# Four tiles of the first diffusion moved to the head of the second step, with the arrays of X and V exchanged and the first layer's loop reordered

## The chip, the cores and the metric

The kernel runs on one core of a Trainium2 chip. It is written by hand for each engine: TensorE (PE) multiplies, VectorE (DVE), ScalarE (ACT) and GpSimd (POOL) do the rest, and SyncE (SP) issues nearly all DMAs. The metric is the time of one execution in microseconds (us), measured on the device; of several runs the median counts.

## The reference

Inputs are `x` (2048 x 512, float32) and a sparse `adj` (2048 x 2048). Two blocks follow each other, each with a residual: `x = x + L0(relu(layernorm(x)), adj)` and then `x = x + L1(relu(layernorm(x)), adj)`. `L0` is a quantised graph layer: 4-bit activations by 3-bit weights, ReLU, quantised again, and `adj @ support`. `L1` is this, with `X` = `V` = its input, `S` = `adj`:

```python
S = S + jnp.eye(n, dtype=X.dtype)
R = S / jnp.clip(S.sum(axis=1, keepdims=True), 1e-12)
Z = jnp.zeros_like(X)
Xf, Xa = (X, X)
...
for s in range(STEPS):                      # two steps
    A = _adj_from_feats(Xa, W1, W2, W3)
    Xf = R @ Xf
    Xa = A @ Xa
    Z = Z + (Xf @ U1s[s] + Xa @ U2s[s])
Y = X + Z
mu = Y.mean(axis=-1, keepdims=True)
var = Y.var(axis=-1, keepdims=True)
return (Y - mu) * jax.lax.rsqrt(var + LN_EPS) * gamma + beta
```

`_adj_from_feats` makes logits `(Xa W1) W2 (Xa W3)^T`, 2048 x 2048, keeps in each row the largest ones that together hold 0.9 of the softmax, and takes the softmax of what was kept. So each step has a diffusion by the fixed matrix `R` and an attention by `A`.

## The kernel before, in words

The 2048 rows are 16 tiles (`T`) of 128, in four groups (`NG`) of four (`G`). Every float32 operand of a product is split into a high and a low half of float16, and a product is the sum of three: high by high, high by low and low by high. The arrays `XR` and `VR` (128 partitions, 16 tiles, two halves, 512) hold the right-hand sides: `XR` the attention's `X`, `VR` the diffusion's `V`. `V` starts as `X U11`; the first diffusion makes `V = X U10 + R V` of it and the second `R V`, the sum of the two diffusion terms of `Z`. The program has these stages, by the profile's clock:

- *Quantising* (to about 80 us): the layer norm of `x`, the first layer's support `sup`, the split weights.
- *The first layer* (80 to 358 us): a loop over 16 strips of `adj`. For strip `t` ACT makes the high half (`adj_hi`), VectorE the sums of its rows (`key_sums`, line 1310), its low half (line 1313) and the block on its diagonal (`own_block`), TensorE the products with `sup` (lines 658 and 665) and, last of a tile, the one-column product of line 668. VectorE then normalises (lines 1348 to 1360) and writes `XF`; ACT (`x_hi`, line 987) and GpSimd (`x_lo`, line 521) split it into `XR`, TensorE turns the halves (line 700) and makes `U10`, `U11` and the logits' factors of the tile before (`post0` on ACT, lines 1018 and 1021; `pk_lo`, `v_lo` on GpSimd, lines 529 to 536). SP writes the turned and split strip to `adj_parts` in DRAM.
- *Step 1* (358 to 946 us) and *step 2* (946 to 1400 us), each the same program with other constants: a head, then four groups.
- *The end* (1400 to 1460 us): the last layer norm and the output.

In a step, the logits of a group (`logits`, lines 756 and 757 on TensorE, copied by ACT at line 1061, squares at 1068) come two groups ahead, tile by tile. VectorE takes the largest of each row (line 1469, four tiles of a group), ACT the four Exps (`terms`, line 1088), VectorE searches the threshold in four rounds of sums over all four tiles (line 1382), sorts out the last candidates and writes the kept terms and their sums (`settle`, lines 1559 to 1662). TensorE turns the kept terms (line 684), ACT copies their high (1119) and low half (1125), and TensorE multiplies them by `XR` (lines 830 and 833). ACT writes the product out (1148 in step 1, 1152 in step 2). In step 1 the new `X` then goes through `U20`, the new `Phh`, `Plz`, `Khl` (the logits' factors) and `x_parts` in DRAM.

A tile of the diffusion is 48 matmuls (lines 778 and 780) of a strip of `adj_parts`, which SP brings in, by `VR`. ACT scales it out of the bank (`r_out`, line 1100), GpSimd adds the term of before (`r_sum`, line 565), and in step 1 ACT and GpSimd split the sum into halves (lines 1104 and 536), which SP stores to `v_parts`. `VR` can't take the new `V` before the old one is read for the last time, so `V` comes back from DRAM: `v_in` reloads `VR` ahead of the last group's pairs in step 1, `x_in` reloads `XR` at the head of step 2.

The order is written out by hand and each engine runs its part of it. `step_order` puts the logits of group 0, its Exps, one diffusion tile, the logits of group 1 and diffusion tiles 1 to 8 ahead of the groups (`R_FIRST = 9`), and each group begins with `R_BEHIND = (1, 2, 2, 2)` further ones, the last of them behind the turning of the first kept terms. ACT's `group_start` does

```python
                e_hi(t + s * T, 0)
                e_hi(t + s * T, 1)
                if g < NG - 1:
                    terms(s, g + 1)
                    r_out(s, first_r(g) + count - 1, bank_of(g, count - 1))
```

so all four Exps of the next group stand there together. On VectorE the loop over the groups is `first_guess` (with `largest`, the four reductions, at its head), `search`, `settle`. A wait for a semaphore stands on the engine that needs the data; everything behind it in that engine's program waits with it.

## Time and profile before

| | us |
|---|---|
| three runs | 1462.3, 1460.14, 1460.16 |
| median | 1460.16 |
| profiled execution, its own time | 1462.12 |
| its span | 1460.3 |
| TensorE matmuls busy | 1217.0 (83%) |
| VectorE busy | 1098.2 (75%) |
| ACT busy | 611.0 (42%) |
| GpSimd busy | 292.6 (20%) |

The mean clock granted to TensorE is 0.937 of full speed. DMAs move 141.78 MB. The span is the time between the first and the last instruction on the core; the execution's own time is 1.8 us more. A busy share is an average over stages with different limits: the two engines that are busy most are rarely busy to the full at the same time. How long something waits and what ended the wait is read from the timeline of its engine.

### The profile page before, as it was taken

The numbers are of one execution on the slowest core, as the hardware profiler recorded it, in microseconds if no ns is written. First come the engines' busy times: TensorE is split into PE (matmuls) and PEld (weight loads), VectorE is DVE, ScalarE is ACT, GpSimd is POOL, SyncE is SP. The second block draws the span as 40 slices with busy tenths as digits, with TensorE's granted clock in tenths as the row PEclk, the third lists the DMA queues.
The fourth block names the chain that finished last, engine by engine and source line by source line (L and its number), as shares of the span: only waits on it lengthen the run. The fifth ranks groups of instructions, "written<-read, shape, count | busy, mean of one in ns | idle before, by whom it ended". The sixth has DMA issues, their size and how long they took to land.

```text
span 1460.3 us, 18002 instructions
## 1 busy us (share of the span) xinstructions
PE 1217.0 (83%) x6042; PEld 591.4 (40%) x6042; DVE 1098.2 (75%) x1864; ACT 611.0 (42%) x1164; POOL 292.6 (20%) x236
## 2 busy tenths in 40 slices
PE   0658888887779989989989999879999849689792
PEld 0324443443224445445445545424445325345351
DVE  7877666663389899869959800079999999999958
ACT  1635343332771255465544334494046236243130
POOL 6024333332022211121121210101111101102111
PEclk9989999998889999999999999989999979889996
DMA  6134444441214410020030040153440210111165
GB/s 218 49 132 169 166 168 151 173 152 60 88 51 154 156 44 30 32 85 15 31 101 16 30 166 15 45 208 103 157 137 30 66 51 29 66 51 44 44 225 178
DMA packets 57395, 141.78 MB, mean 97 GB/s; under 512 B 9632, under 2 KB 9632, under 8 KB 53216
## 3 DMA queue, kind: packets, MB, share of 16 engines
q1 hardware_dynamic: 57312, 140.81, 27.8%
q8 instruction: 36, 0.59, 0.2%
q14 instruction: 47, 0.39, 0.1%
HBM read 89.67 MB, written 51.12 MB: 96 GB/s over the span
## 4 chain that ended last, share of the span: by engine, by line
PE 46%; DVE 22%; issue 11%; POOL 8%; ACT 8%; DMA 3%; SPq 1%; DVEq 1%; POOLq 1%; ACTq 0%
DVE WS L1382 7%; PE UB L675 6%; PE AB L830 4%; PE AB L778 4%; PE RB L830 4%; PE AB L665 3%; PE RB L675 3%; PE XB L675 3%; PE RB L778 2%; POOL Plz L529 2%; ACT E L1088 2%; POOL RT L565 2%; PE AB L833 2%; PE AB L780 2%; DVE w L1596 2%
## 5 line engine op out<-in xcount | busy, mean ns | idle before, releaser
L1382 DVE SCALAR_TENSOR_TENSOR WS<-E,g 128x2048 bf16<-128x2048 f32 x128 | 315.4, 2515 | 2.0 <-ACT E L1088 0.8
L1469 DVE TENSOR_REDUCE g<-E 128x1 f32<-128x2048 f32 x32 | 72.9, 2278 | 143.1 <-ACT E L1061 143.1
L684 PE MATMUL TB<-ident,E 128*128 128x128 f32 x512 | 81.2, 287 | 72.8 <-ACT turns L1125 45.1
L1125 ACT ACTIVATE turns<-TB 128x512 f16<-128x512 f32 x128 | 75.3, 594 | 155.0 <-PE TB L690 154.8
L830 PE MATMUL AB<-XR,turns 128*128 128x512 f16 x512 | 130.3, 401 | 0.0
L565 POOL TENSOR_TENSOR RT<-RT,AD 128x512 f32<-128x512 f32 x32 | 55.2, 1725 | 361.3 <-ACT RT L1100 361.3
L830 PE MATMUL RB<-XR,turns 128*128 128x512 f16 x512 | 121.0, 379 | 0.0
L778 PE MATMUL RB<-VR,AH 128*128 128x512 f16 x512 | 115.6, 385 | 0.0
L778 PE MATMUL AB<-VR,turns 128*128 128x512 f16 x512 | 114.1, 379 | 0.0
L684 PEld LDWEIGHTS TB<-ident,E 128*128 128x128 f32 x512 | 66.4, 148 | 98.8 <-issue 48.6
L1119 ACT ACTIVATE turns<-TB 128x512 f16<-128x512 f32 x128 | 75.4, 593 | 34.6 <-PE TB L684 34.6
L1559 DVE SCALAR_TENSOR_TENSOR E<-E,g 128x2048 f32<-128x2048 f32 x33 | 79.2, 2432 | 12.6 <-issue 12.4
L665 PE MATMUL AB<-E,turns 128*128 128x512 f16 x256 | 67.1, 410 | 23.3 <-DVE turns L1313 23.3
L580 POOL TENSOR_TENSOR XHL<-WF,XHL 128x512 f16<-128x512 f32 x16 | 28.3, 1768 | 280.2 <-ACT XHL L1140 280.2
L1061 ACT ACTIVATE E<-LB 128x512 f32<-128x512 f32 x128 | 75.6, 599 | 18.8 <-PE LB L757 17.3
L756 PE MATMUL LB<-Khl,Phh 128*128 128x512 f16 x128 | 53.9, 421 | 33.7 <-ACT E L1061 26.0
L1088 ACT ACTIVATE E<-E,nmx 128x2048 f32<-128x2048 f32 x32 | 63.7, 1997 | 31.5 <-DVE nmx L1470 31.5
L778 PEld LDWEIGHTS RB<-VR,AH 128*128 128x128 f16 x512 | 50.7, 99 | 61.3 <-issue 4.0
L830 PEld LDWEIGHTS AB<-XR,turns 128*128 128x128 f16 x512 | 52.5, 103 | 56.5 <-issue 9.9
L778 PEld LDWEIGHTS AB<-VR,turns 128*128 128x128 f16 x512 | 50.1, 98 | 59.8 <-issue 0.4
L1596 DVE MAX8 w<-WS 128x8 f32<-128x2048 f32 x32 | 73.4, 2295 | 1.1
L598 POOL TENSOR_TENSOR UO<-UO,Khl 128x512 f32<-128x512 f32 x16 | 32.5, 2032 | 204.2 <-ACT UO L1152 150.5
(292 smaller groups left out, 2245.5 us busy)
## 6 DMA issues: line engine op xcount, KB each, us to landing
turns<-adj_parts SPq DMA_DIRECT2D x48, 512.0 KB, 3.8
E<-adjT SPq DMA_DIRECT2D x16, 1024.0 KB, 5.1
adj_parts<-turns SPq DMA_DIRECT2D x16, 1024.0 KB, 3.9
AH<-adj_parts SPq DMA_DIRECT2D x16, 512.0 KB, 3.7
z_d<-UO SPq DMA_DIRECT2D x31, 256.0 KB, 2.3
XR<-x SPq DMA_DIRECT2D x4, 1024.0 KB, 12.0
WS<-U SPq DMA_DIRECT2D x4, 1024.0 KB, 5.6
x_d<-E SPq DMA_DIRECT2D x16, 256.0 KB, 2.6
```

The lines of the kernel that those rows point to most:

```text
L565: q.tensor_tensor(RT[:, :], RT[:, :], AD[:, :], ALU.add).then_inc(s_rsum, 1)
L665: mm(AB[:, :], turns[:, h, 1, j, :], sup[:, j, :], start=False, stop=(j == T - 1))
L675: i = mm(dst, a(k), b(k), start=(first and n == 0), stop=(last and n == 3 * KC - 1))
L684: i = mm(bank[:, k * P:(k + 1) * P], src(k), ident32[:, :], is_transpose=True, start=(k == 0), stop=(k == KC - 1), skip_group_check=True)
L778: i = mm(bank[:, :], at_hi[odd][:, j, :], VR[:, j, k % 2, :], start=(k == 0), stop=False)
L830: mm(bank[:, :], ET[:, 0, j, :], XR[:, j, y_, :], start=(j == 0 and y_ == 0), stop=False)
L1061: a(E[:, slot, c * CH:(c + 1) * CH], LB[c % 2][:, :], ACT.Copy, scale=1.0 / (SV * SV), accum_out=ls[:, bass.ds(slot, 1), c:c + 1].rearrang ...
L1088: a(E[:, slot, :], E[:, slot, :], ACT.Exp, bias=nmx[:, slot:slot + 1], accum_out=tot[:, slot:slot + 1]).then_inc(s_exp, 1)
L1119: a(ET[:, 0, c * KC:(c + 1) * KC, :].rearrange("p b c -> p (b c)"), TB[c % 2][:, :], ACT.Copy, scale=SE).then_inc(s_eh, 1)
L1382: return v.scalar_tensor_tensor(junk[t % 2], e, g4[:, k, t:t + 1], e, op, ALU.mult, accum_out=g4[:, F_, t:t + 1])
L1559: return v.scalar_tensor_tensor(E[:, slot, :], E[:, slot, :], g4[:, k, t:t + 1], E[:, slot, :], ALU.is_ge, ALU.mult, accum_out=g4[:, DEN, ...
L1596: ct(v.max(w8[:, t, :], WS[:, :]))
```

## The change

Three things change. (1) Step 1 runs 12 tiles of the first diffusion, step 2 the other four (`R_LATE`) ahead of its own. The arrays trade places: at the head of step 2 `v_in` loads the first 12 tiles of `V` into `XR`, ACT and GpSimd write the last four straight into `XR`, and the second diffusion reads `XR`; `x_in` loads `X` into `VR` once tile 15 of the first diffusion has been read, and the attention of step 2 reads `VR`. All diffusion tiles of a group now stand ahead of its turning, 0, 1, 1, 1 in step 1 and 1, 3, 4, 3 in step 2. (2) The Exps of the next group are divided: two (`EARLY`) in `group_start`, two in the group's tile 0 behind the squares. VectorE does two of the next group's reductions between `search` and `settle`. (3) In the first layer VectorE sums strip `t + 1`, makes its low half and its own block before it waits for the product of strip `t`; ACT's high half of `t + 1` comes ahead of its copies of the turned x, and its half of x (and GpSimd's) ahead of the rest of the tile before; `key_sums` has two buffers. Ahead of the loop strip 0 is summed between two quantising steps, its high half is made before them, and GpSimd makes a U half before the four roots. SP issues loads and stores in the order that this asks for.

The diff, cut to its core:

```diff
 R_FIRST = 9
-R_BEHIND = (1, 2, 2, 2)
+R_LATE = 4
+EARLY = 2
+R_BEHIND = ((0, 1, 1, 1), (1, 3, 4, 3))
 R_HI = 2 * T
 R_ALL = R_HI + T
...
-        X1T, tmp, key_sums, own = misc[:, 0, :], misc[:, 1, :], misc[:, 2, 0:P], misc[:, 2, P:2 * P]
+        X1T, tmp, own = misc[:, 0, :], misc[:, 1, :], misc[:, 2, 2 * P:3 * P]
+        key_sums = misc[:, 2, 0:2 * P].rearrange("p (h c) -> p h c", h=2)
...
+        def step_order(s, logits, terms, r_one, r_span, group_start, pairs, last_post):
             logits(s, 0)
             terms(s, 0)
-            r_tile(s)
-            logits(s, 1)
-            r_tiles(s, 1, R_FIRST)
+            if s == 0:
+                r_one(0, 0)
+                r_span(0, 1, 3)
+                logits(s, 1)
+                r_span(0, 3, R_FIRST)
+            else:
+                r_one(0, T - R_LATE)
+                r_span(0, T - R_LATE + 1, T - 1)
+                logits(s, 1)
+                r_one(0, T - 1)
+                r_one(1, 0)
+                r_span(1, 1, R_FIRST - R_LATE)
             for g in range(NG):
                 group_start(s, g)
...
+            def l0_tile(t, odd):
+                l0_stores(t)
+                at_out(t + 1, odd)
+                adj_in(t + 3)
+                diag_out(t)
+                post0_stores(t - 1)
+
...
             def v_in():
-                sp.wait_ge(s_vout, 16 * T + OPEN)
+                sp.wait_ge(s_vout, 16 * (T - R_LATE) + OPEN)
+                sp.wait_ge(s_u, 2 * T)
+                sp.dma_start(XR[:, 0:T - R_LATE, :, :].rearrange("p t h d -> p t (h d)"),
+                             v_parts[0:T - R_LATE].rearrange("t p h d -> p t (h d)")).then_inc(s_vr, 16)
+
+            def x_in():
+                sp.wait_ge(s_xout, 16 * T)
                 sp.wait_ge(s_r, T)
                 sp.dma_start(VR[:, :, :, :].rearrange("p t h d -> p t (h d)"),
-                             v_parts.rearrange("t p h d -> p t (h d)")).then_inc(s_vr, 16)
-
-            def x_in():
-                sp.wait_ge(s_xout, 16 * T)
-                sp.wait_ge(s_u, 2 * T)
-                sp.dma_start(XR[:, :, :, :].rearrange("p t h d -> p t (h d)"),
                              x_parts.rearrange("t p h d -> p t (h d)")).then_inc(s_xr, 16)
 
...
             def l0_tile(t):
                 l0(t)
+                x_lo(t, of(XR, t))
                 v_lo(t - 1, of(VR, t - 1))
                 pk_lo(t - 1, 0, t - 1, s_vl, t)
-                x_lo(t, of(XR, t))
...
+                vs = XR if rs else VR
+                if rs and isinstance(t, int) and t == 0 and a == 0:
+                    pe.wait_ge(s_vr, 16)
+                    pe.wait_ge(s_vl, 2 * T + OPEN)
...
+                xs = XR if qq < T else VR
...
                 a(UO[:, :], UB[:, :], ACT.Copy, scale=SV / (SX * SW)).then_inc(s_ue, 1)
+                if more:
+                    x_hi(t + 1)
                 act.wait_ge(s_v, t + 1)
                 act.wait_ge(s_vl, t + OPEN)
                 a(RT[:, :], RB[:, :], ACT.Copy, scale=SV / (SX * SW)).then_inc(s_ve, 1)
...
             def l0_tile(t):
-                xT_halves(t - 1)
                 turn_free(t + 1)
                 adj_hi(t + 1)
+                xT_halves(t - 1)
                 post0(t - 1)
-                x_hi(t)
...
-            def terms(s, g):
+            def terms(s, g, tiles=range(G)):
                 gq = s * NG + g
-                for t in range(G):
+                for t in tiles:
...
+                if rs == 0:
                     act.wait_ge(s_rsum, r + 1)
+                    if late:
+                        act.wait_ge(s_u, 2 * T)
+                        a(XR[:, bass.ds(t, 1), 0, :].rearrange("p o d -> p (o d)"), RT[:, :], ACT.Copy).then_inc(s_vh, 1)
+                    else:
+                        act.wait_ge(s_vout, 16 * t + OPEN)
+                        a(VHL[:, 0, :], RT[:, :], ACT.Copy).then_inc(s_vh, 1)
...
-                a_out(s, g, t, slot, bank_of(g, R_BEHIND[g] + i))
+                if i == 0 and g < NG - 1:
+                    terms(s, g + 1, range(EARLY, G))
+                a_out(s, g, t, slot, bank_of(s, g, R_BEHIND[s][g] + i))
                 if more:
...
                     w_out(t - 1)
+                    if g < NG - 1:
+                        terms(s, g + 1, range(EARLY))
                     pk(t - 1 + T, 1, t - 1, UB)
-                if g:
-                    r_out(s, first_r(g), bank_of(g, 0))
-                if g == NG - 1:
-                    r_out(s, first_r(g) + count - 1, bank_of(g, count - 1))
+                for j, (rs, r) in enumerate(rows):
+                    r_out(rs, r, bank_of(s, g, j))
+                    if s and j == 0 and g < NG - 1:
+                        terms(s, g + 1, range(EARLY))
+                if s + g == 0:
+                    terms(s, 1, range(EARLY))
                 e_hi(t + s * T, 0)
                 e_hi(t + s * T, 1)
-                if g < NG - 1:
-                    terms(s, g + 1)
-                    r_out(s, first_r(g) + count - 1, bank_of(g, count - 1))
...
+            def adj_sums(t):
+                dve.wait_ge(s_raw, 16 * t + 16)
+                v.tensor_reduce(key_sums[:, t % 2, :], raw[:, t % 2, :].rearrange("p (j c) -> p c j", j=T), AX.X,
+                                ALU.add).then_inc(s_part, 1)
+
+            def adj_lo(t):
+                dve.wait_ge(s_ah, t + 1)
+                v.scalar_tensor_tensor(turns[:, t % 2, 1, :, :].rearrange("p t c -> p (t c)"), raw[:, t % 2, :], SA,
+                                       turns[:, t % 2, 0, :, :].rearrange("p t c -> p (t c)"), ALU.mult,
+                                       ALU.subtract).then_inc(s_al, 1)
+
+            quantise_x(0)
+            quantise_x(1)
+            adj_sums(0)
+            quantise_support(0)
+            quantise_x(2)
+            quantise_support(1)
+            quantise_x(3)
+            quantise_support(2)
+            wpk_parts(ch)
+            quantise_support(3)
+            adj_lo(0)
+
...
-            def layer0(t, first=False):
+            def layer0(t, last=False):
                 ct = Chain(dve, c_dve, t * per0 + base)
-                adj_lo(t)
-                own_block(t, ct)
-                if first:
-                    wpk_parts(ct)
+                if not last:
+                    adj_sums(t + 1)
+                    adj_lo(t + 1)
+                    own_block(t + 1, ct)
...
-                    first_guess(g, g + s * NG, ct)
-                    search(g, g + s * NG, ct)
-                    settle(g, g + s * NG, ct)
+                    gq = g + s * NG
+                    if g == 0:
+                        largest(g, gq, ct, slice(0, EARLY))
+                    largest(g, gq, ct, slice(EARLY, None))
+                    first_guess(g, gq, ct)
+                    search(g, gq, ct)
+                    if g < NG - 1:
+                        largest(g + 1, gq + 1, ct, slice(0, EARLY))
+                    settle(g, gq, ct)
```

The first place is VectorE's program around the first layer's loop (the first rows are the end of quantising; `L1310` is the sum of a strip, `L1313` its low half, `L1333` to `L1336` the own block, `L1348` to `L1360` the layer norm down to `XF`). Before:

```order
L1297 TENSOR_SCALAR E<-VR 128x2048
L1310 TENSOR_REDUCE E<-E 128x128
L1313 SCALAR_TENSOR_TENSOR turns<-E,turns 128x2048
L1333 TENSOR_TENSOR E<-E,ident 128x128
L1335 TENSOR_SCALAR diag<-E 128x128
L1336 SCALAR_TENSOR_TENSOR diag<-E,diag 128x128
L1348 TENSOR_SCALAR sc<-LB 128x1
L1359 TENSOR_SCALAR E<-E,mv,sc 128x512
L1360 TENSOR_SCALAR XF<-E 128x512
L1364 COPY sc<-sc 128x1
L1366 UNCONDITIONAL_BRANCH
```

After, where the same lines are 1351, 1356, 1379 to 1382 and 1394 to 1406, and the branch is the head of the loop:

```order
L1356 SCALAR_TENSOR_TENSOR turns<-E,turns 128x2048
L1379 TENSOR_TENSOR E<-E,ident 128x128
L1381 TENSOR_SCALAR diag<-E 128x128
L1382 SCALAR_TENSOR_TENSOR diag<-E,diag 128x128
L1411 UNCONDITIONAL_BRANCH
L1351 TENSOR_REDUCE E<-E 128x128
L1356 SCALAR_TENSOR_TENSOR turns<-E,turns 128x2048
L1379 TENSOR_TENSOR E<-E,ident 128x128
L1381 TENSOR_SCALAR diag<-E 128x128
L1382 SCALAR_TENSOR_TENSOR diag<-E,diag 128x128
L1394 TENSOR_SCALAR sc<-LB 128x1
L1406 TENSOR_SCALAR XF<-E 128x512
```

The sum, low half and block of the next strip stand in the loop ahead of the row that reads the product (`L1394`), and those of strip 0 ahead of the loop.

The second place is ACT's program at the start of group 0 in step 2 (`RT` is a diffusion tile, `E,tot` an Exp, `turns` the halves of kept terms, `squares` those of the logits, `UO` the product of attention tile 0). Before:

```order
L1119 ACTIVATE turns<-TB 128x512 x2
L1088 ACTIVATE E,tot<-E,nmx 128x2048 x4
L1100 ACTIVATE RT<-RB,rinv 128x512
L1125 ACTIVATE turns<-TB 128x512 x2
L1061 ACTIVATE E,ls<-LB 128x512 x2
L1061 ACTIVATE E,ls<-LB 128x512 x2
L1068 ACTIVATE squares,lq<-E 128x1024 x2
L1152 ACTIVATE UO<-AB,rden 128x512
```

After (`L1130` is the diffusion's copy, `L1118` the Exp, `L1154` and `L1160` the two halves, `L1098` the squares, `L1187` the product):

```order
L1130 ACTIVATE RT<-RB,rinv 128x512
L1118 ACTIVATE E,tot<-E,nmx 128x2048 x2
L1154 ACTIVATE turns<-TB 128x512 x2
L1160 ACTIVATE turns<-TB 128x512 x2
L1091 ACTIVATE E,ls<-LB 128x512 x2
L1091 ACTIVATE E,ls<-LB 128x512 x2
L1098 ACTIVATE squares,lq<-E 128x1024 x2
L1118 ACTIVATE E,tot<-E,nmx 128x2048 x2
L1187 ACTIVATE UO<-AB,rden 128x512
```

Two of the four Exps stand ahead of the halves, the other two behind the squares and ahead of the product of tile 0.

The third place is TensorE's program at the end of step 2's head (`LB` is a logits' bank, `RB` and `AB` take diffusion tiles, `TB` turned terms). Before:

```order
L778 MATMUL AB<-VR,turns 128x512 x32
L780 MATMUL AB<-VR,turns 128x512 x16
L805 REGISTER_ALU
L805 COMPARE_AND_BRANCH
L684 MATMUL TB<-ident,E 128x128 x8
L778 MATMUL RB<-VR,AH 128x512 x32
L780 MATMUL RB<-VR,turns 128x512 x16
L690 MATMUL TB<-turns,minus_e 128x512 x2
```

After:

```order
L782 MATMUL LB<-Khl,Phh 128x512
L783 MATMUL LB<-Khl,Plz 128x512
L790 REGISTER_ALU
L790 COMPARE_AND_BRANCH
L808 MATMUL RB<-VR,AH 128x512 x32
L810 MATMUL RB<-VR,turns 128x512 x16
L808 MATMUL AB<-XR,turns 128x512 x32
L810 MATMUL AB<-XR,turns 128x512 x16
L808 MATMUL RB<-XR,AH 128x512 x32
L810 MATMUL RB<-XR,turns 128x512 x16
L808 MATMUL RB<-XR,AH 128x512 x32
L810 MATMUL RB<-XR,turns 128x512 x16
L710 MATMUL TB<-ident,E 128x128 x8
L716 MATMUL TB<-turns,minus_e 128x512 x2
```

Tile 15 of the first diffusion (by `VR`) and tile 0 of the second (by `XR`) follow each other, the loop reads `XR`, and no diffusion tile stands any more between the turning of terms and the taking off of their high halves (`TB<-turns,minus_e`).

## Rows read from the trace of the kernel before

**Rows 1.** Stretches: start:end, us, busy us of PE, PEld, DVE, ACT, POOL, granted clock, DMA, GB/s.

```profile
80.00:347.00 267.00, 222.82 (x1166) 107.27 (x1167) 181.63 (x237) 99.82 (x161) 93.45 (x75) 0.94 0.43 158
504.00:946.00 442.00, 415.64 (x2176) 212.95 (x2174) 286.70 (x534) 212.21 (x440) 76.85 (x64) 0.97 0.15 51
...
1084.00:1380.00 296.00, 239.43 (x1161) 120.42 (x1161) 280.72 (x509) 115.71 (x225) 38.61 (x19) 0.91 0.16 51
```

**Rows 2.** Instructions of line 668: count, least, median and most ns, first and last start.

```profile
L668 PE MATMUL LB<-powc,E x32: 167/209/250, 90.4 to 347.1; 128*128 128x1 f32 x32
```

**Rows 3.** Timeline, TensorE, first layer: start us, us, instruction [idle before <-releaser].

```profile
193.69 0.28 PE L668 MATMUL LB<-powc,E 128*128 128x1 f32 x2
199.68 3.62 PE L658 MATMUL AB<-E,turns 128*128 128x512 f16 x16
204.40 1.04 PE L665 MATMUL AB<-E,turns 128*128 128x512 f16 x4 [1.11 <-DVE turns L1313]
206.86 1.11 PE L700 MATMUL XB<-ident,XR 128*128 128x128 f16 x8 [1.42 <-POOL XR L521]
```

**Rows 4.** Timeline, first layer: VectorE, then ACT, then GpSimd.

```profile
98.25 4.60 DVE L1313 SCALAR_TENSOR_TENSOR turns<-E,turns  x1
...
197.88 0.43 DVE L1360 TENSOR_SCALAR XF<-E 128x512 f32<-128x512 f32 x1
202.07 2.28 DVE L1313 SCALAR_TENSOR_TENSOR turns<-E,turns  x1
...
201.50 0.27 ACT L1018 ACTIVATE Khl<-XB 64x128 f32 x1
208.92 1.90 ACT L987 ACTIVATE turns<-E  x1
...
202.25 2.38 POOL L529 TENSOR_TENSOR Plz<-PKf,Phh 64x128 f32 x1 [0.25 <-POOL VR L536]
```

**Rows 5.** Timeline, TensorE, the end of the first layer.

```profile
358.08 1.01 PE L700 MATMUL XB<-ident,XR 128*128 128x128 f16 x8 [4.83 <-POOL XR L521]
```

**Rows 6.** Timeline, head and groups of step 1: TensorE, then ACT, then VectorE.

```profile
386.82 7.07 PE L778 MATMUL AB<-VR,turns 128*128 128x512 f16 x32
410.34 0.61 PE L756 MATMUL LB<-Khl,Phh 128*128 128x512 f16 x1 [12.13 <-ACT E L1061]
521.09 1.09 PE L684 MATMUL TB<-ident,E 128*128 128x128 f32 x4 [5.43 <-ACT turns L1125]
603.68 0.63 PE L684 MATMUL XB<-ident,XF 128*128 128x128 f32 x4 [1.41 <-ACT XF L1148]
860.74 0.76 PE L684 MATMUL TB<-ident,E 128*128 128x128 f32 x4 [0.29 <-ACT turns L1125]
...
539.13 0.67 ACT L1148 ACTIVATE XF<-AB,rden 128x512 f32<-128x512 f32 x1
...
516.33 2.35 DVE L1382 SCALAR_TENSOR_TENSOR WS<-E,g 128x2048 bf16<-128x2048 f32 x1
596.52 2.35 DVE L1559 SCALAR_TENSOR_TENSOR E<-E,g 128x2048 f32<-128x2048 f32 x1 [1.22 <-issue]
```

**Rows 7.** Groups of instructions by line, whole program: busy us, mean ns, idle before.

```profile
L565 POOL TENSOR_TENSOR RT<-RT,AD 128x512 f32<-128x512 f32 x32 | 55.2, 1725 | 361.3 <-ACT RT L1100 361.3
...
L1061 ACT ACTIVATE E<-LB 128x512 f32<-128x512 f32 x128 | 75.6, 599 | 18.8 <-PE LB L757 17.3
...
L1061 ACT ACTIVATION_READ_ACCUMULATOR E<-LB 128x1 f32 x128 | 26.2, 205 | 0.0
...
L1088 ACT ACTIVATE E<-E,nmx 128x2048 f32<-128x2048 f32 x32 | 63.7, 1997 | 31.5 <-DVE nmx L1470 31.5
```

**Rows 8.** Timeline, start of step 2's group 0: TensorE, VectorE, ACT.

```profile
1084.97 0.63 PE L684 MATMUL TB<-ident,E 128*128 128x128 f32 x4 [0.93 <-ACT turns L1125]
...
1080.82 2.35 DVE L1382 SCALAR_TENSOR_TENSOR WS<-E,g 128x2048 bf16<-128x2048 f32 x1
...
1100.30 0.67 ACT L1152 ACTIVATE UO<-AB,rden 128x512 f32<-128x512 f32 x1
```

320 lines of the change are left out of this document (156 added, 164 removed).

## The prediction, made before the changed kernel ran

> **What bounds the kernel now.** I read the table of stretches first, because one share of busy time says nothing here [rows 1]. From 80 to 347 us (the first layer) TensorE is busy 83% and no engine is full. From 504 to 946 (groups of step 1) TensorE has 416 of 442 us and VectorE 287. From 1084 to 1380 (groups of step 2) it is the reverse: VectorE 281 of 296, TensorE 239. So the same 10 us of matmuls cost time in step 1 and nothing in step 2, as long as they fit into TensorE's 57 idle us there. Then I read the places where the bound changes hands.
>
> *First layer.* The matmul that ends a tile comes first at 90.4 and last at 347.1 [rows 2], 15 periods of 17.1 us. In one of them [rows 3] TensorE waits 1.1 us for VectorE's low half and 1.4 us for GpSimd's low half of x; the cause stands in [rows 4]: after XF (197.88) VectorE still sums the next strip and only then, at 202.07, makes its low half.
>
> *Step 1.* TensorE resumes with tiles at 521.09 after a wait of 5.4 and with those of the last group at 860.74 [rows 6].
>
> *Step 2.* VectorE's search runs without a hole, because ACT has made all four Exps of the next group before [rows 8].
>
> **The change, part by part.** All is counted in the profiled execution (1462.1 us).
>
> *1. First layer, loop.* VectorE now does the sums, low half and own block of strip t+1 before it waits for product t. TensorE's own work per tile: from the end matmul 6.0 us to the next high product (193.69 to 199.68), 16 high and 16 low matmuls at 0.216 each (3.62 = 15 pitches + 0.38), 6.9, eight turnings 0.94: 13.9 us. Do the others keep up? ACT's last copy of keys ends 8.1 us after the end matmul [rows 4]; the copy of x now stands before them, in idle time; then the next high half 1.9, which makes 10.0; low half on VectorE 2.3, 12.4; own block about 1, 13.4. The next end matmul comes at 13.9. It just fits, so I take 13.9. The first period is shorter: the strip is ready, and TensorE has no products of a tile before; it ends with the chain XF, halves of x, turning, about 11.0. With 1.5 for the two U halves that VectorE and GpSimd still fight over: 11.0 + 14 x 13.9 + 1.5 = 207.1 against 256.7. **-49.6.** The moves ahead of it (strip 0 summed while VectorE waits, W parts in another wait, U before the four roots) add 3.7 us of VectorE work to the quantising and take as much from its end; first high product within 1 us of before: 0, range -3 to +2.
>
> Every third tile of before is longer (17.1 on average against 16.7 in the one shown). The Trainium skill (TensorE: Matmul & The Clock Gate, What's actually happening) says that idleness puts the array at 1.2 GHz and activity returns it to 2.4. By that, a loop without waits loses these dips, as in my 13.9; by the row they would stay, 0.4 x 14 = +6, which I keep for the upper end.
>
> *2. Its end.* The last x was turned at 358.08, 11.0 after the last end matmul, behind GpSimd's work on the tile before [rows 5]. Now x goes first; the next in line is ACT, which is busy until +8.1 and then copies the turned x. Before it did that from +12.0. **-3.7.**
>
> *3. Head of step 1.* Before, TensorE did one diffusion tile, then waited 12.1 us in the logits [rows 6] for ACT's four Exps. Now diffusion tiles 1 and 2 stand there. A diffusion tile is 48 x 0.216 = 10.36. In before's clock: three tiles from 386.8 end at 417.9, plus 1.2 for a late transfer; ACT finishes their sums at 422.2; 16 copies of logits at 0.8 (599 + 205 ns) [rows 7] to 434.8; six tiles to 497.0. ACT then needs 0.7 + 1.7 (GpSimd) + 0.6, and the two early Exps 4.0 [rows 7], to 504.3; TensorE resumes with tiles at 506.2, not 521.09. Tile 9, which stood between, is gone from there. **-14.9.** VectorE's first tile is ready at 500.1 (its old 495.3 and two early reductions of 2.4), so it isn't last.
>
> *4. Groups of step 1.* Each group has one diffusion tile fewer, 10.4 us. But what is late next? The search of a group starts in step 1 only with all four Exps, and the last two now stand in ACT's queue behind the squares of tile 0: 18.0 us after TensorE resumes (521.09 to 539.13), then 4.0, then 0.5. From search to first masked tile 80.2 (516.33 to 596.52) [rows 6], plus 4.8 for two early reductions, plus 3.0 until TensorE resumes: 110.5. For the third hand-over tile 0 has no logits, so ACT gets there after 13, and no reduction follows: 100.7. Sum of three: 321.7, against 860.74 - 521.09 = 339.7. **-18.0.** TensorE alone would need 82.6 (to 603.68) + 3.4 for a late copy + 17.3 of tile and rest + 7 = 110.3, so the two are level, and the gain is less than 3 x 10.4 because the wait for the Exps takes the rest. The last group's missing tile lies before 860.74 and is in this sum.
>
> *5. Head of step 2.* Ten diffusion tiles stand before the first turning (12 to 15 of the first, 0 to 5 of the second), nine did. New is a wait: tile 0 of the second needs all V, so after tile 15 TensorE idles for ACT 0.7, GpSimd 1.7, ACT 0.6, GpSimd 1.7 and hops, 5.1. In before's clock: three tiles from 958.6 to 989.7; ACT is behind with three sums, so the logits end at 1005.6; tile 15 to 1016; wait to 1021; six tiles, the first partly cold, 1084.4. ACT: 0.7, then the two early Exps 4.0, both halves: TensorE resumes at 1091, not 1084.97 [rows 8]. X into VR (4 MB) is issued at about 1018 beside this; a strip's transfer may be 2 late. GpSimd's and SP's queues hold the same items in the new order.
>
> *6. The hand-over in step 2.* This is the term against the change. VectorE is done with two reductions, moments and the first two sums of the search at 1080.8, as before. The third needs Exp 3, and that stands in ACT's queue behind the squares of tile 0, 15.3 after TensorE resumes (1084.97 to 1100.30) [rows 8]: 1091 + 15.3 + 2 = 1108, where before it began at 1080.82. **+27.5**, and step 2 is bound by VectorE, so it stays. Later hand-overs: TensorE has 3, 4 and 3 diffusion tiles (31, 41, 31) before the group's turning. After 57.5 of tiles and 31 it is at 1182, VectorE's mask at 1190; then ACT is blocked some 10 us until the late reductions, tiles and 41 end at 1304 against the mask at 1310; then 1398 against 1407. So the four moved tiles lie beside VectorE's work, by 6 to 9 us each time, and cost 0. If that cover is gone, each us is one. The last groups' tail is unchanged.
>
> Sum: -49.6 - 3.7 - 14.9 - 18.0 + 27.5 = -58.7, which makes 1403.4 for an execution like the profiled one; the median of the runs is 2.0 below it: 1401.5, say **1402**.
>
> **The rivals.** *A. The first layer keeps most of its waits.* Its ring VectorE, ACT, VectorE fits with 0.5 us to spare. VectorE's low half took 4.60 instead of 2.28 where GpSimd worked beside it, and GpSimd's Plz 2.38 [rows 4]. If low half and own block meet GpSimd in each tile, the ring is 12.4 + 2.3 + 2.4 = 17.1, no gain; if only the block does, 15.3. For it: two slow rows. Against: in the new order GpSimd's operations start with x at +5.4 and end by +9.3, before the low half. 14 x 1.4 to 14 x 3.2 gives 1422 to 1447. The Trainium skill (GPSIMD Engine Reference, Specifications) states the cause: GpSimd shares its SBUF interfaces with VectorE instructions that have two SBUF inputs, which both are.
>
> *B. No hand-over stall in step 2*, if the two Exps were reached before VectorE asks: 1402 - 27.5 = 1374. Against: the order itself puts squares ahead of them.
>
> *C. Slower than before: TensorE at its lower level.* After the change TensorE is nearly full in some 730 us (207, then 505, then the head of step 2). Its mean granted clock there was 0.94 to 0.97 [rows 1]. From 8% more time in these stretches (58.7 / 730), a mean of about 0.89, all gain is lost. At 0.84, 730 x (0.96 / 0.84 - 1) = +104: 1506. For it: denser work. Against: the stretch 504 to 946 is the densest and has the highest clock, 0.97.
>
> **How the numbers follow.** My forecast gets 61% (own range 1388 to 1418: the 6 us of dips, 5 on each ring, 3 ahead), A 25%, B 9%, C 5%. The range 1384 to 1430 takes in the lower part of A and leaves out B, the rest of A and C. A measurement of this kernel can tell about 0.2% (3 us) from no change. Faster: all but C, 0.95; a change within 3 us needs A in full and a longer stall, 0.01; slower 0.04.
>
> **What would show it.** In the profile after: end matmuls of the first layer 13.9 apart, the last near 297; TensorE's resuming in the last group of step 1 some 86 earlier (860.74 - 53.3 - 32.9 = 774.5); one hole of 25 to 30 us on VectorE in the second search of step 2, released by ACT's Exp; none of that size in the others; 5 us on TensorE before the second diffusion's tile 0. I am wrong if the period is over 15, if VectorE has holes of 10 or more in the two later hand-overs, or if TensorE makes VectorE's masked tiles wait.

## The result and the profile after

The changed kernel takes **1415.16 us** (median of 4 runs, 1413.95 to 1416.03) against 1461.14 before (median of 4). The ratio is 0.9684, 95% interval 0.9668 to 0.9701: 46 us, or 3.2%, faster. The forecast was 1402, its range 1384 to 1430, so the time lies inside, 13 us above the likeliest value. The profiled execution took 1413.95 us, with a span of 1412.2. The comparisons inside the program below are made between this profile and that of before, whose spans differ by 48.1.

The end matmuls of the first layer, which answer [rows 2], and the stretches that answer [rows 1] (start:end, length, busy us of PE, PEld, DVE, ACT, POOL, granted clock, share of DMA, GB/s):

```profile
L694 PE MATMUL LB<-powc,E x32: 167/208/251, 88.0 to 295.8; 128*128 128x1 f32 x32
```

```profile
80.00:296.00 216.00, 207.15 (x1168) 104.14 (x1167) 157.99 (x229) 99.93 (x160) 66.77 (x75) 0.98 0.57 195
504.00:860.00 356.00, 331.08 (x1752) 171.03 (x1749) 252.35 (x459) 170.84 (x360) 57.03 (x51) 0.97 0.10 35
1045.00:1330.00 285.00, 250.56 (x1200) 122.55 (x1198) 270.86 (x488) 100.11 (x188) 35.06 (x21) 0.94 0.22 69
```

TensorE is now busy 96% of the first layer, where it was 83%, and the granted clock there went from 0.94 to 0.98. One whole tile of the loop, TensorE first, then VectorE, then ACT, all in one period of 13.34 (end matmul to end matmul, the pattern of [rows 3, 4]):

```profile
181.65 3.62 PE L684 MATMUL AB<-E,turns 128*128 128x512 f16 x16
185.10 1.03 PE L691 MATMUL AB<-E,turns 128*128 128x512 f16 x4
185.97 0.61 PE L726 MATMUL XB<-ident,XR 128*128 128x128 f16 x8
189.00 0.28 PE L694 MATMUL LB<-powc,E 128*128 128x1 f32 x2
```

```profile
179.87 0.43 DVE L1406 TENSOR_SCALAR XF<-E 128x512 f32<-128x512 f32 x1
180.56 3.74 DVE L1351 TENSOR_REDUCE E<-E  x1 [0.20 <-issue]
185.85 2.29 DVE L1356 SCALAR_TENSOR_TENSOR turns<-E,turns  x1 [1.56 <-ACT turns L1005]
...
183.76 1.91 ACT L1005 ACTIVATE turns<-E  x1
```

No row of TensorE carries a wait: the low half that VectorE makes at 185.85 is that of the *next* strip. VectorE's and ACT's waits have no one behind them.

Step 2 is where the change costs. First the row of TensorE ahead of the second diffusion's tile 0, then ACT, VectorE and TensorE at the start of group 0, which answer [rows 8]:

```profile
938.84 0.58 PE L808 MATMUL AB<-XR,turns 128*128 128x512 f16 x1 [6.29 <-POOL XR L562]
...
1003.48 0.69 ACT L1130 ACTIVATE RT<-RB,rinv 128x512 f32<-128x512 f32 x1 [9.49 <-PE RB L810]
1004.06 1.99 ACT L1118 ACTIVATE E<-E,nmx 128x2048 f32<-128x2048 f32 x1
1008.03 1.06 ACT L1154 ACTIVATE turns<-TB 128x512 f16<-128x512 f32 x2
...
1027.89 1.99 ACT L1118 ACTIVATE E<-E,nmx 128x2048 f32<-128x2048 f32 x1
1031.86 0.67 ACT L1187 ACTIVATE UO<-AB,rden 128x512 f32<-128x512 f32 x1
...
1006.18 2.35 DVE L1430 SCALAR_TENSOR_TENSOR WS<-E,g 128x2048 bf16<-128x2048 f32 x1 [7.81 <-ACT E L1118]
1030.07 2.35 DVE L1430 SCALAR_TENSOR_TENSOR WS<-E,g 128x2048 bf16<-128x2048 f32 x1 [19.26 <-ACT E L1118]
...
1008.67 1.10 PE L716 MATMUL TB<-turns,minus_e 128*128 128x512 f16 x2 [4.36 <-ACT turns L1154]
1010.05 1.09 PE L710 MATMUL TB<-ident,E 128*128 128x128 f32 x4 [0.29 <-ACT turns L1160]
1010.94 3.62 PE L863 MATMUL AB<-VR,turns 128*128 128x512 f16 x8
...
1115.33 1.97 PE L710 MATMUL TB<-ident,E 128*128 128x128 f32 x8 [10.77 <-DVE E L1607]
```

VectorE, the engine that bounds this stage, stands idle twice in one search, 27.1 us in all: before its first sum, for the first Exp, and before its third, for the third, which ACT makes at 1027.89 behind the squares of tile 0. ACT itself waited 9.49 for the last diffusion tile just before the first of these Exps.

Place by place, the same events in both profiles:

| event | before | after | difference | step since the row above | forecast of the step |
|---|---|---|---|---|---|
| first end matmul of the first layer | 90.4 | 88.0 | -2.4 | -2.4 | 0 |
| last end matmul | 347.1 | 295.8 | -51.3 | -48.9 | -49.6 |
| first sum of step 1's search | 405.57 | 351.14 | -54.4 | -3.1 | -3.7 |
| TensorE resumes, group 0 of step 1 | 521.09 | 456.95 | -64.1 | -9.7 | -14.9 |
| TensorE resumes, last group of step 1 | 860.74 | 777.42 | -83.3 | -19.2 | -18.0 |
| TensorE resumes, group 0 of step 2 | 1084.97 | 1010.05 | -74.9 | | |
| third sum of group 1's search, step 2 | 1080.82 | 1030.07 | -50.8 | +32.5 | +27.5 |
| end of the span | 1460.3 | 1412.2 | -48.1 | +2.7 | 0 |

(The forecast's sum of -58.7 is that of the last column.) Without the first layer's part, which earned 54.4 with its lead-in and end, the change costs 6.3 by this table: -9.7 - 19.2 + 32.5 + 2.7. The same by stages: from the first sum of its first search to that of step 2's, step 1 takes 537.4 instead of 566.4, and from there to the last group's first masked tile step 2 takes 439.3 instead of 404.0.

### The profile page after: what moved, and what is told of

It is laid out like the page before. It is cut to its first block, busy times and chain, and to the rows that moved or that the text cites. A ratio compares the mean times of both kernels' runs of the same rounds, so it can differ in the third digit from the quotient of the medians.

```text
span 1412.2 us, 17981 instructions
## 1 busy us (share of the span) xinstructions
PE 1211.1 (86%) x6042; PEld 589.8 (42%) x6042; DVE 1091.7 (77%) x1863; ACT 613.0 (43%) x1164; POOL 273.7 (19%) x236
## 4 chain that ended last, share of the span: by engine, by line
PE 42%; DVE 28%; issue 12%; ACT 9%; DMA 4%; POOL 3%; SPq 1%; DVEq 1%; POOLq 0%; ACTq 0%
DVE WS L1430 10%; PE UB L701 6%; PE RB L863 3%; PE AB L863 3%; PE AB L691 3%; PE AB L684 3%; PE XB L701 3%; ACT E L1118 3%; PE RB L701 3%; DVE w L1644 3%; PE RB L808 2%; PE TB L710 2%; POOL RT L591 2%; DMA AD<-xu_d 2%; PE AB L808 2%
## 5 line engine op out<-in xcount | busy, mean ns | idle before, releaser
L1430 DVE SCALAR_TENSOR_TENSOR WS<-E,g 128x2048 bf16<-128x2048 f32 x128 | 315.1, 2512 | 28.2 <-ACT E L1118 27.1
L1160 ACT ACTIVATE turns<-TB 128x512 f16<-128x512 f32 x128 | 75.7, 594 | 148.9 <-PE TB L716 148.7
L1154 ACT ACTIVATE turns<-TB 128x512 f16<-128x512 f32 x128 | 75.6, 594 | 39.0 <-PE TB L710 38.9
L716 PE MATMUL TB<-turns,minus_e 128*128 128x512 f16 x128 | 52.0, 410 | 33.4 <-ACT turns L1154 33.4
L624 POOL TENSOR_TENSOR UO<-UO,Khl 128x512 f32<-128x512 f32 x16 | 28.5, 1780 | 253.7 <-ACT UO L1187 195.9
L782 PE MATMUL LB<-Khl,Phh 128*128 128x512 f16 x128 | 57.0, 445 | 21.0 <-ACT E L1091 14.0
L684 PE MATMUL AB<-E,turns 128*128 128x512 f16 x256 | 61.3, 395 | 11.9 <-DVE E L1335 5.9
L1098 ACT ACTIVATE squares<-E 128x1024 bf16<-128x1024 f32 x64 | 67.6, 1056 | 2.6
L1118 ACT ACTIVATE E<-E,nmx 128x2048 f32<-128x2048 f32 x32 | 63.6, 1990 | 5.9 <-DVE nmx L1514 5.9
L808 PE MATMUL AB<-XR,turns 128*128 128x512 f16 x256 | 58.8, 390 | 6.3 <-POOL XR L562 6.3
L863 PE MATMUL AB<-VR,turns 128*128 128x512 f16 x256 | 63.4, 393 | 0.0
L1351 DVE TENSOR_REDUCE E<-E (+1 forms) x16 | 59.6, 3723 | 3.0 <-issue 3.0
L863 PE MATMUL AB<-XR,turns 128*128 128x512 f16 x256 | 61.9, 385 | 0.0
L863 PE MATMUL RB<-XR,turns 128*128 128x512 f16 x256 | 61.7, 385 | 0.0
```

What stands on the lines that cost most here:

```text
L684: mm(AB[:, :], turns[:, h, 0, j, :], sup[:, j, :], start=(j == 0), stop=False)
L808: i = mm(bank[:, :], at_hi[odd][:, j, :], vs[:, j, k % 2, :], start=(k == 0), stop=False)
L863: mm(bank[:, :], ET[:, 0, j, :], xs[:, j, y_, :], start=(j == 0 and y_ == 0), stop=False)
L1118: a(E[:, slot, :], E[:, slot, :], ACT.Exp, bias=nmx[:, slot:slot + 1], accum_out=tot[:, slot:slot + 1]).then_inc(s_exp, 1)
L1154: a(ET[:, 0, c * KC:(c + 1) * KC, :].rearrange("p b c -> p (b c)"), TB[c % 2][:, :], ACT.Copy, scale=SE).then_inc(s_eh, 1)
L1160: a(ET[:, 1, c * KC:(c + 1) * KC, :].rearrange("p b c -> p (b c)"), TB[c % 2][:, :], ACT.Copy, scale=SE).then_inc(s_et, 1)
```

## The experiments

Eleven more kernels ran. All medians below are those of a kernel's own 4 or 5 runs, and before was run beside them (medians from 1460.3 to 1462.7).

| kernel | us | ratio to before, 95% interval |
|---|---|---|
| changed kernel | 1415.16 | 0.9684 (0.9668 to 0.9701) |
| first layer's part alone | 1409.17 | 0.9632 (0.9608 to 0.9657) |
| all but the first layer's part | 1472.13 | 1.0082 (1.0050 to 1.0113) |
| changed, four Exps in ACT's gap | 1390.12 | 0.9506 (0.9484 to 0.9528) |
| changed, four Exps behind the copy | 1396.87 | 0.9564 (0.9526 to 0.9602) |
| changed, head of step 1 undone | 1418.58 | 0.9686 (0.9646 to 0.9726) |
| changed, loads first | 1410.88 | 0.9636 (0.9592 to 0.9681) |
| changed, 1, 5, 3, 2 tiles in step 2 | 1419.66 | 0.9691 (0.9649 to 0.9732) |
| gap, loads first, two more | 1387.12 | 0.9473 (0.9434 to 0.9512) |
| gap, loads first | 1383.37 | 0.9470 (0.9450 to 0.9490) |
| the same, late Exps at once | **1372.55** | 0.9402 (0.9386 to 0.9418) |
| the same, two late tiles | 1392.77 | 0.9521 (0.9497 to 0.9546) |

### The two halves of the change by themselves

*The first layer's part alone*: before, with part (3) of the change and nothing else (the pieces of the diff on `key_sums`, `l0_tile`, `post0`, `adj_sums`, `own_block`, `layer0`, and the order of SP's first loads).

> Before with part (3) of the change alone: the first layer's loop and what leads into it. Theory by the stages of the changed profile: first layer, its lead-in and its end gave 54.4 us, the two steps together cost 6.3. So 1461.1 - 54.4 = 1407 (1404 to 1410), faster than the whole change by about 8. Rival, by the sum of the prediction: the steps' part is worth -5.4 (-14.9 - 18.0 + 27.5), so this kernel would be slower than the whole change: 1420.

Measured: 1409.17 (1407.15 to 1412.01), 52.9 below the 1462.08 of before beside it. It is as the theory has it, and faster than the whole change: the two intervals of the ratio don't touch.

*All but the first layer's part*: the changed kernel with exactly those pieces undone.

> Before with everything but the first layer's part: four late tiles, exchanged arrays, divided Exps. Theory: 1461.1 + 6.3 = 1467 (1464 to 1471), slower than before. Rival by the sum of the prediction: 1461.1 - 5.4 = 1456. A third: the steps' part only looks bad behind a shorter first layer, then 1461 or less.

Measured: 1472.13 (1465.59 to 1478.3), 10 above before, ratio 1.0050 to 1.0113. That is 1 above the theory's range, with a spread of 13 between its runs; its profiled execution was the fastest, at 1465.6, and its span is 3.5 above that of before. So the part that gives the change its name makes this kernel slower, by 10 in the medians and 3.5 in the profiles. The rival that took the sum of the prediction's terms falls, and the third with it. Which of the two, the moved tiles or the divided Exps, brings the loss, this kernel doesn't say; it holds both.

### Where the loss in step 2 is

*Four Exps in ACT's gap*: the Exps of group 1 of step 2 change their place in ACT's program (first in its `tile`, then in its `group_start`).

```diff
-                if i == 0 and g < NG - 1:
+                if i == 0 and g < NG - 1 and (s, g) != (1, 0):
                     terms(s, g + 1, range(EARLY, G))
...
+                if (s, g) == (1, 0):
+                    terms(1, 1)
                 for j, (rs, r) in enumerate(rows):
                     r_out(rs, r, bank_of(s, g, j))
-                    if s and j == 0 and g < NG - 1:
+                    if s and g and j == 0 and g < NG - 1:
                         terms(s, g + 1, range(EARLY))
```

> The changed kernel, with all four Exps of group 1 of step 2 ahead of ACT's copy of the last diffusion tile of the head, where ACT idles 9.5 us; nothing else. Theory (the Exps' place in ACT's queue makes both holes of VectorE, 7.8 and 19.3): holes gone, later hand-overs keep their cover of 6 to 9, so 1415.2 - 27 = 1388 (1385 to 1392), and TensorE's wait of 10.8 for the second mask shrinks to under 1. Rival (TensorE takes over as soon as VectorE is 27 earlier): 1400 to 1408, with TensorE full through groups 1 and 2 and VectorE waiting for late Exps in one of them.

Measured: 1390.12 (1389.7 to 1392.44), 25.0 less than the changed kernel. The same rows in its profile (ACT, then VectorE):

```profile
999.42 0.69 ACT L1130 ACTIVATE RT<-AB,rinv 128x512 f32<-128x512 f32 x1 [9.69 <-PE AB L810]
1000.01 1.99 ACT L1118 ACTIVATE E<-E,nmx 128x2048 f32<-128x2048 f32 x1
1001.99 1.99 ACT L1118 ACTIVATE E<-E,nmx 128x2048 f32<-128x2048 f32 x1
1003.98 1.99 ACT L1118 ACTIVATE E<-E,nmx 128x2048 f32<-128x2048 f32 x1
1005.96 1.99 ACT L1118 ACTIVATE E<-E,nmx 128x2048 f32<-128x2048 f32 x1
1009.60 0.69 ACT L1130 ACTIVATE RT<-RB,rinv 128x512 f32<-128x512 f32 x1 [1.56 <-PE RB L810]
...
1004.43 2.34 DVE L1432 SCALAR_TENSOR_TENSOR WS<-E,g 128x2048 bf16<-128x2048 f32 x1
1006.70 2.35 DVE L1432 SCALAR_TENSOR_TENSOR WS<-E,g 128x2048 bf16<-128x2048 f32 x1
1008.97 2.35 DVE L1432 SCALAR_TENSOR_TENSOR WS<-E,g 128x2048 bf16<-128x2048 f32 x1
```

The first, second and third sum follow each other without a wait, four Exps lie where ACT had idled, and the copy at 1009.60 still waits 1.56 for TensorE, so that nothing was delayed by them. From the search of group 0 to the last mask step 2 takes 412.6 (894.62 to 1307.17) instead of 439.3 (888.50 to 1327.77): 26.7, the size of the two holes. So 27 us of the stall lay on the path in full, and TensorE did not take over. What is left of the loss in step 2 is 8.5 (412.6 against 404.0 in before), the size of the later resuming of TensorE at its head; no experiment took that apart.

*Four Exps behind the copy*: as this, but behind `r_out` of the head's last tile.

> The changed kernel, with all four Exps of group 1 of step 2 behind that copy instead of ahead of it. Theory: the hole of 7.8 before the first sum stays, the one of 19.3 goes; ACT's halves of tile 0 come 4 later, which TensorE has covered by its wait for the second mask: 1415.2 - 19.3 = 1396 (1393 to 1399). Rival (the 4 us on TensorE is paid): 1400. Rival (the price of the stall is only partly on the path): over 1405.

Measured: 1396.87, with a wide spread: two runs at 1392 and two at 1401, and the profile is of the fastest. It has the hole of 7.8 before the first sum and not the one before the third:

```profile
1003.08 2.35 DVE L1430 SCALAR_TENSOR_TENSOR WS<-E,g 128x2048 bf16<-128x2048 f32 x1 [7.82 <-ACT E L1118]
...
1009.54 1.09 PE L716 MATMUL TB<-turns,minus_e 128*128 128x512 f16 x2 [8.33 <-ACT turns L1154]
```

TensorE waits 8.33 for its first halves where it had waited 4.36, and the step is not longer for it: 421.0 from the first sum to the last mask, which is the 412.6 of the kernel above with a hole of 7.8. In the profile the theory's place and price hold; between 1396 and the 1400 of the first rival the times don't decide.

*1, 5, 3, 2 tiles behind the groups of step 2.*

```diff
-R_BEHIND = ((0, 1, 1, 1), (1, 3, 4, 3))
+R_BEHIND = ((0, 1, 1, 1), (1, 5, 3, 2))
```

> The changed kernel with diffusion tiles 1, 5, 3, 2 behind the groups of step 2 instead of 1, 3, 4, 3: two more tiles (20.7 us of TensorE) ahead of the second turning, where TensorE waits 10.8 for VectorE's mask. Theory (VectorE is the bound, the cover is what TensorE waits): TensorE 10 late in group 1, its late Exps at 1151 to 1155 against VectorE's wish of 1152, so +1 to +3: 1417. Rival (each us of TensorE behind the cover is paid): +10, 1425.

Measured: 1419.66 (1416.63 to 1424.7), 4.5 more, where the theory had 1 to 3. In its profile step 2 takes 442.0 from the first sum to the last mask (896.10 to 1338.05), 2.7 more than in the changed kernel; the rest is no more than the 8 us by which its runs differ. Two more tiles stand ahead of the second mask, 20.7 us of TensorE, and they cost 2.7: the wait for the mask is their cover, as the prediction's term 6 said, and VectorE is the bound.

### The head of step 1

*The head in the old order.*

```diff
                 r_one(0, 0)
-                r_span(0, 1, 3)
                 logits(s, 1)
-                r_span(0, 3, R_FIRST)
+                r_span(0, 1, R_FIRST)
```

> The changed kernel, with the head of step 1 in the old order: diffusion tiles 1 and 2 behind the logits of group 1. Theory from the changed profile: the first six turnings' place moved from 503.8 - 54.4 = 449.4 to 446.5, so the two tiles gave 2.9 and not the 6.8 of the prediction (503.8 to 497.0); the rest of what step 1's head gave is tile 9, which is gone from between the turnings. Undone: 1415.2 + 2.9 = 1418 (1416 to 1420). Rival (the prediction's own count): +6.8, 1422. Rival (the 12 us wait never cost anything): 1415.

Measured: 1418.58 (1416.88 to 1420.73), +3.4. The ratio's interval (0.9646 to 0.9726) is too wide to part +2.9 from +6.8 or from nothing by time. The profiles do it: from the first sum of step 1's first search to TensorE's first turning are 98.3 us in before (405.57 to 503.83) and 98.3 here (351.76 to 450.05), and in the five kernels with the new order and the old queue 94.6 to 97.7, the changed kernel's 95.4 among them. So the two tiles gave 0.6 to 3.7.

*Loads first.* Why less than 6.8? In the changed profile TensorE waits in the third diffusion tile; TensorE, then SP's queue around it:

```profile
363.90 4.96 PE L810 MATMUL AB<-VR,turns 128*128 128x512 f16 x16 [3.72 <-DMA turns<-adj_parts]
373.83 0.61 PE L782 MATMUL LB<-Khl,Phh 128*128 128x512 f16 x1 [4.11 <-ACT E L1091]
```

```profile
342.95 0.33 SPq L360 DMA_DIRECT2D turns<-adj_parts  x1
354.64 0.33 SPq L364 DMA_DIRECT2D AD<-xu_d  x1
357.80 0.34 SPq L372 DMA_DIRECT2D v_parts<-VHL  x1
358.51 0.36 SPq L356 DMA_DIRECT2D AH<-adj_parts  x1
359.06 0.33 SPq L360 DMA_DIRECT2D turns<-adj_parts  x1
```

Tile 1 was finished at about 353.1 and the low half of strip 2 could have been loaded then. It was issued at 359.06, behind `AD` and the store of the first tile's `V`. These two wait for GpSimd, whose sum of tile 0 ends at 354.6 and whose low half at 357.8, and GpSimd waits for ACT, which makes four Exps until 350.6. The edit takes the loads of the next two strips ahead (SP's program):

```diff
             def r_one(rs, t):
+                if (rs, t) == (0, 0):
+                    at_hi_in(0, 2, 0)
+                    at_lo_in(0, 1)
+                    at_hi_in(0, 3, 1)
+                    at_lo_in(0, 2)
+                    ad_in(0, 1)
+                    r_store(0, 0, False)
+                    ad_in(0, 2)
+                    r_store(0, 1, False)
+                    return
...
-                if a == T - R_LATE + 1:
+                if (rs, a, b) == (0, 1, 3):
+                    r_done(0, 2, 0)
+                elif a == T - R_LATE + 1:
```

> The changed kernel, with the two next strips' halves issued on SP's queue ahead of the store of the first diffusion tile's V, which waits for ACT. Theory: TensorE's wait of 3.7 to 4 us in diffusion tile 2 is that queue order, and it lies on the path through ACT's copies of the logits: 1415.2 - 3.8 = 1411.4, TensorE's first wait in step 1's group 0 starts about 4 earlier. Rival (the DMAs are slow there, not late): no change in that wait. Rival (the path goes through VectorE's first masks): the wait goes, the time stays.

Measured: 1410.88 (1407.48 to 1414.31), -4.3, but the intervals of the two ratios overlap. In the profile TensorE's wait for the strip is gone, and step 1 takes 533.9 from search to search, where the changed kernel takes 537.4. This is the firmer number: this kernel and the two below that add the gap to it take 533.8 to 534.1, the five with the old queue and the new head 536.7 to 540.8. What is late next is VectorE's kept terms, for which TensorE now waits 4.87 at 448.15: the second rival has a part of it, since that wait would eat any further gain there.

### How far it goes

*Gap, loads first, and two more*: in step 1 the early Exps ahead of the last two copies of the head, and the late Exps ahead of the squares.

> The kernel with the Exps in the gap (1390.1), and three more of the kind: loads first (-3.8), in step 1 the two early Exps ahead of ACT's copies of the last two diffusion tiles of the head instead of behind them (-4.0, they stand between the last tile and the first halves), and the late Exps of each hand-over ahead of the squares instead of behind (2.4 each, three times in step 1, where VectorE waits 16, 7 and 3 for them; at most what TensorE waits for masks: 3, 3 and 8). Theory: 1390.1 - 3.8 - 4.0 - 5 = 1377 (1374 to 1382). Rival (TensorE is full in step 1, what comes earlier from ACT is not used): 1384 to 1387.

Measured: 1387.12 (1386.18 to 1388.77): the rival's time. Step 1 takes 534.1, as with loads first alone. The early Exps did come sooner, at 426.80, and the masks, not they, held TensorE at 448.50. Without the two:

> The kernel with the Exps in the gap, and the loads first on SP's queue; neither of the other two parts of the kernel with all. Theory after that run (its step 1 took 534.1 against 533.9 with the loads first alone, so the other two parts gave nothing): 1390.1 - 3.8 = 1386.3 (1384 to 1388), the same as all three within 1. Rival (one of the two parts did give and the other cost): over 1389 or under 1384.

Measured: 1383.37 (1380.04 to 1387.31), 3 under the theory, below its range and just inside the rival's. The two ratios, 0.9473 and 0.9470, are the same, and the runs spread over 7 us, so the times don't decide. The profiles speak for the rival, one part that gave and one that cost. With the two parts the first hand-over of step 1 is 5.2 us shorter from search to search (117.2 against 122.4) and the second 5.9 longer (115.3 against 109.4). The edit also moved the late Exps in step 2, where the theory had counted nothing, and there the time from the first sum to the last mask is 2.6 longer (415.1 against 412.6).

*Late Exps at once.*

```diff
                     e_lo(qq, 1)
                     e_hi(qq, 2)
+                    if s == 0 and g < NG - 1:
+                        terms(s, g + 1, range(EARLY, G))
                 e_lo(qq, 2)
...
-                if i == 0 and g < NG - 1 and (s, g) != (1, 0):
+                if s and i == 0 and 0 < g < NG - 1:
                     terms(s, g + 1, range(EARLY, G))
```

> As the one with gap and loads, and in step 1 the two late Exps of a hand-over stand behind the third high half of tile 0 instead of behind its squares: some 12 us earlier. Theory: step 1's period of 109.2 is a ring (masks, turning, late Exps, search), in which TensorE waits 3.1 for masks and 3.1 behind the late Exps, and VectorE 7.4 for them. With the Exps at once VectorE searches 12 earlier, TensorE waits for no mask, and pays some 2.5 once in tile 0: per group -3 to -4, so step 1 takes 526 (523 to 530) instead of 534 and the whole 1379 (1376 to 1382). Rival (TensorE's own work is the bound, 106 with its waits for ACT): -2 or less, over 1384. Rival (ACT's 4 us in tile 0 stop TensorE in full each time): no gain or a loss, over 1386.

Measured: **1372.55** (1370.8 to 1376.66), 10.8 less than without it, more than forecast. Step 1 takes 520.4 from search to search (352.55 to 872.96), 13.4 less. First VectorE's wait for the late Exps in the changed kernel's first hand-over; then this kernel's profile, ACT and TensorE in tile 0, and the larger of the two waits of VectorE for an Exp that are left in step 1's hand-overs (the other is 2.3):

```profile
477.26 0.16 DVE L1557 SCALAR_TENSOR_TENSOR g<-tot,g 128x4 f32<-128x4 int32 x1 [16.26 <-ACT E L1118]
...
457.75 2.00 ACT L1130 ACTIVATE E<-E,nmx 128x2048 f32<-128x2048 f32 x1 [3.31 <-DVE nmx L1530]
460.13 2.00 ACT L1130 ACTIVATE E<-E,nmx 128x2048 f32<-128x2048 f32 x1 [0.29 <-DVE nmx L1530]
...
463.25 0.39 PE L728 MATMUL TB<-turns,minus_e 128*128 128x512 f16 x1 [1.19 <-ACT turns L1166]
...
669.84 0.16 DVE L1573 SCALAR_TENSOR_TENSOR g<-tot,g 128x4 f32<-128x4 int32 x1 [4.62 <-ACT E L1130]
```

TensorE waits 1.2 behind the late Exps where it waited 3.1, and at the three hand-overs it no longer waits for a mask (at two of them it now waits 4.3 and 3.3 for ACT's first halves instead). Its first turnings of the four groups are 105.3, 105.1 and 97.0 apart, where without the edit they are 112.4, 109.4 and 101.8: 16.3 less, or 5.4 for each on average where I had forecast 3 to 4, and 3 of it are lost again behind the last. The first hand-over gives most, 7.1; why it gives more than forecast is open.

So step 1 was a ring through three engines: masks free TensorE, TensorE's work frees ACT, and ACT's Exps free the search that makes the masks. Neither of the two busy engines was full: from 477.67 to 691.71 of the changed kernel TensorE has 199.3 of 214.0 and VectorE 192.4, and here from 463 to 670 they have 195.8 and 190.1 of 207.0. This is the fastest kernel of the study: 6.0% under before (5.8 to 6.1), 43 us under the changed kernel.

*Two late tiles instead of four*, on top of it.

```diff
-R_LATE = 4
+R_LATE = 2
...
-R_BEHIND = ((0, 1, 1, 1), (1, 3, 4, 3))
+R_BEHIND = ((0, 1, 2, 2), (1, 2, 3, 3))
...
-                r_span(0, T - R_LATE + 1, T - 1)
```

> As the one with the late Exps at once (1372.6), but with two late tiles instead of four: 14 diffusion tiles in step 1 (0, 1, 2, 2 behind the groups), and 1, 2, 3, 3 in step 2. Theory: in step 1 TensorE is now the bound, so the two tiles that come back cost their full 10.4 each; in step 2, where VectorE is the bound, two tiles fewer give 0 to 2. So 1372.6 + 20 = 1392 (1388 to 1394). Rival (the four late tiles earn nothing themselves, the order of the Exps and the first layer do): 1371 to 1376. Rival (a ring again, half of it is hidden): 1380 to 1385.

Measured: 1392.77 (1392.06 to 1395.21), +20.2. From search to search step 1 takes 539.4 (352.36 to 891.76), 19.0 more, 9.5 for each tile that comes back. So in step 1 the tiles are worth nearly their whole length, once the order of the Exps lets it through. In step 2 the comparison isn't clean. The theory had 0 to 2 less there, and in the profiles it takes 4.7 more from the first sum to the last mask (417.0 against 412.3), with a new hole of VectorE, because the copy ahead of the Exps comes later now:

```profile
1007.00 2.35 DVE L1445 SCALAR_TENSOR_TENSOR WS<-E,g 128x2048 bf16<-128x2048 f32 x1 [12.41 <-ACT E L1129]
```

A two-tile kernel with its Exps placed for it was not made, so the 20.2 is the price of the two tiles with this order, not of the tiles alone.

## Why the prediction was right, and where it was off

The time lies in the range because the first layer's part, by far the largest term, came out as forecast in sum. The part that the change is named for did not: terms 3 to 6 promised a gain of 5.4 and are a loss of 6.3 in the profiles. The signs named beforehand came nearly all: the last end matmul at 295.7 (297 forecast), TensorE in step 1's last group at 777.4 (774.5), VectorE idle 27.1 in the second search of step 2 and without such a hole in the later hand-overs, though in two pieces and not one.

1. *First layer, loop*: right in sum, -48.9 against -49.6, and that close by luck, since neither number in it was right: the twelve steady periods are 6.7 shorter than forecast in all and the first three 7.3 longer. The period of the twelve steady tiles is 13.34, not 13.9: I had added the turnings' 0.94 as a whole, and the eight take TensorE 0.44 here (185.97 to 186.41). The clock isn't the reason, since 1.00 was granted in before too while they took 0.94 (206.86 to 207.80); there they stand behind a wait for GpSimd's half of x, and why that makes them longer is open. The first three periods are 14.88, 14.14 and 18.57. The third was not in the forecast: ACT makes a half of `U` there (two passes of 1.91) ahead of the high half of the strip, and the low half then took 4.37 beside GpSimd's 4.06 on the same `U`. Rival A falls: the low half is 2.29 in the steady tiles, and GpSimd is done by 185.2, before it starts. The low half of 4.60 in before, which the Trainium skill's GPSIMD Engine Reference explains (Specifications), was an exception there as well: it stood beside GpSimd's 4.06 on a half of `U`, and 14 of before's 16 low halves took 2.27 to 2.29. The clock dips went. The long third periods of before had a granted clock of 0.90 (227.11 to 244.85, 17.74 us) and the others 1.00; now the steady periods have 1.00 and one length. The Trainium skill (TensorE: Matmul & The Clock Gate, What's actually happening) says that the array is throttled by idleness and released by activity, and the trace agrees.
2. *Its end*: -3.1 against -3.7; right.
3. *Head of step 1*: -9.7 against -14.9, the first term that was mis-sized. I gave 1.2 for a late transfer and not for what stood ahead of it on SP's queue: TensorE waits 3.7. The rest is the lower clock behind that wait (the 16 low matmuls took 4.96 and not 3.62), and with it later logits.
4. *Groups of step 1*: -19.2 against -18.0; the ring was seen, with intervals of 109.2, 109.2 and 102.1 for forecast ones of 110.5, 110.5 and 100.7. That another place of the late Exps would cut step 1 by 13.4 us wasn't in the text.
5. *Head of step 2*: TensorE resumes 8.4 later relative to the groups before (-83.3 to -74.9), 6.0 in the forecast. The wait before the second diffusion's first tile is 6.3 (forecast 5.1), since GpSimd's sum and half took 2.0 and 2.4 where I had 1.7 for each.
6. *The hand-over in step 2*: +32.5 against +27.5, the second mis-sized term. The mechanism is as written, in two holes instead of one, and the run with the Exps in the gap shows that it is the cause: 25 us. What I missed is 2.4 from point 5, and 2.7 in tile 0, whose first eight matmuls took 3.62 and not 1.89 (the row of TensorE in [rows 8] has 0.9 of wait, now it is 4.4). The hole before the first sum wasn't seen: I took the first two Exps to be ready as before, and they come at 1004.06. Later hand-overs have no hole, as forecast. The 2.7 that follow I can place only in part: from there to the last mask VectorE's sums last 2.501 on average, 2.479 before, which makes 1.0 for 46 of them.

The lead-in's 2.4 isn't the change's: in the ten other profiles with the new first layer the first end matmul comes at 90.0 to 91.9, close to that of before (90.4). That -48.1 in the profiles is -46.0 in the times has another reason: the profiled execution is 1.2 below the median of the changed kernel and 1.0 above that of before. Rival B (no stall) and C (slower, by a lower clock) fall; the clock of the whole went from 0.937 to 0.942. That the change as named is a loss by itself did not follow from my terms: the sum of 3 to 6 is a gain of 5.4, and what turned its sign are the 5.2 of the head of step 1, the 5.0 of the hand-over and the 2.7 behind it, less 1.2 that the groups of step 1 gave over the forecast.

Open: by how much the changed head of step 1 pays (0.6 to 3.7 in the profiles), what the moved tiles would cost or give with the Exps undivided, and what makes the runs of one kernel differ by 2 to 13 us here, where those of before differ by 2 to 10.
